# First attention of a four-part kernel: loads, statistics and moments of four batch entries in the set-up, those of the other 28 inside its first four steps, mask row on ScalarE

## What is computed

```python
x = x + _L0_xattn_ref(ctx_1024, _layernorm(x, axis=-1), mask, ...)   # the stage changed here
x = x + _L0_ffn_ref(_layernorm(x, axis=-1), ...)
x = x + _L1_xattn_ref(_layernorm(x, axis=-1), ctx_1024, ctx_1024, ...)
x = x + _L1_ffn_ref(x, ...)                # latent attention and a mixture of experts

def _L0_xattn_ref(x, latents, mask, ...):  # x is the context here, latents the tokens
    x, latents = layer_norm(x, ...), layer_norm(latents, ...)
    q = latents @ Wq
    k, v = split(concat([x, latents]) @ Wkv)
    q, k = l2norm(q) * q_scale, l2norm(k) * k_scale          # per head
    sim = where(full_mask, (q @ k.T) * 8, max_neg)           # mask over the 120 context keys
    return layer_norm((softmax(sim) @ v) @ Wo, ln_o_w, ln_o_b)
```

## Time and profile before

| | us |
|---|---|
| median of three runs (lowest, highest) | 1343.3 (1341.84, 1346.9) |
| the profiled execution | 1344.71 |
| its span, first to last instruction | 1342.9 |
| PE busy | 1228.8 (92%) |
| DVE busy | 927.4 (69%) |
| ACT busy | 798.7 (59%) |
| POOL busy | 590.4 (44%) |

### The profile page before, as it was taken

The page is one execution under the profiler, slowest core; times in us unless marked ns, Lnnn a source line. Parts: engine busy times, 40 slices in busy tenths (PEclk is TensorE's granted clock), DMA queues, the critical chain, the costliest instruction groups (busy, mean ns, idle before and its releaser), DMA issues. The chain is left out here.

```text
span 1342.9 us, 37984 instructions
## 1 busy us (share of the span) xinstructions
PE 1228.8 (92%) x13719; PEld 879.0 (65%) x13719; DVE 927.4 (69%) x1995; ACT 798.7 (59%) x2101; POOL 590.4 (44%) x677
## 2 busy tenths in 40 slices
PE   1799999999999995969999999599999979999996
PEld 0466666666666663437777777488888847777775
DVE  6476776776776773757989989399999956333431
ACT  0578778778778862216777777266666633333332
POOL 3587566566566555013233232543333224333343
PEclk9899999999999997988999999599999979999998
DMA  8000000000000000000000000200000000000000
GB/s 210 17 1 1 0 0 0 0 0 0 0 0 0 0 1 1 0 6 10 10 7 11 10 7 6 64 3 0 0 0 0 2 1 9 9 8 8 8 10 16
DMA packets 22740, 14.71 MB, mean 11 GB/s; under 512 B 6378, under 2 KB 21610, under 8 KB 22540
## 3 DMA queue, kind: packets, MB, share of 16 engines
q1 hardware_dynamic: 22520, 13.75, 3.9%
q10 hardware_dynamic: 148, 0.01, 0.0%
HBM read 11.66 MB, written 2.10 MB: 10 GB/s over the span
## 5 line engine op out<-in xcount | busy, mean ns | idle before, releaser
L694 POOL TENSOR_TENSOR r_norm<-ssm,mhalf 128x24 f32<-128x24 f32 x32 | 134.9, 4214 | 161.5 <-DVE ssm L599 161.5
L1938 ACT ACTIVATE moe_hid<-psum 128x512 f32<-128x512 f32 x128 | 76.4, 598 | 137.9 <-PE psum L1872 137.9
L537 ACT ACTIVATE l_probs<-psum,l_n_max 128x248 f32<-128x248 f32 x256 | 117.2, 481 | 57.5 <-DVE l_n_max L617 57.5
L2096 POOL TENSOR_TENSOR moe_acc<-moe_acc,moe_prod 128x512 f32<-128x512 f32 x64 | 81.3, 1271 | 147.8 <-DVE moe_prod L2052 147.8
L1882 PEld LDWEIGHTS psum<-w,moe_hid 128*128 128x128 f32 x1024 | 123.1, 192 | 27.0 <-issue 27.0
L2052 DVE TENSOR_TENSOR moe_prod<-psum,moe_combine 128x512 f32<-128x512 f32 x64 | 44.3, 692 | 136.2 <-PE psum L1882 136.1
L1882 PE MATMUL psum<-w,moe_hid 128*128 128x128 f32 x1024 | 123.4, 275 | 0.0
L1872 PE MATMUL psum<-moe_moe_hT,w 128*128 128x512 f32 x256 | 122.9, 608 | 0.0
L1726 POOL TENSOR_TENSOR mla_QX<-mla_qT,own_slots 128x512 f32<-128x512 f32 x32 | 33.3, 1042 | 136.0 <-ACT mla_qT L1560 136.0
L701 POOL TENSOR_TENSOR qkn<-qk,r_norm 128x1536 f32<-128x1536 f32 x32 | 88.4, 2762 | 2.5
L1726 POOL TENSOR_TENSOR l_QX<-l_qT,own_slots 128x512 f32<-128x512 f32 x32 | 33.3, 1042 | 122.3 <-ACT l_qT L1560 122.3
(11 more groups left out here) (311 smaller groups left out, 3393.2 us busy)
## 6 DMA issues: line engine op xcount, KB each, us to landing
X<-x_in SPq DMA_DIRECT2D x8, 256.0 KB, 4.9
out_dram<-moe_acc SPq DMA_DIRECT2D x32, 64.0 KB, 1.5
CT<-ctx_in SPq DMA_DIRECT2D x8, 240.0 KB, 6.1
l_cT<-ctxT_in SPq DMA_DIRECT2D x32, 60.0 KB, 1.8
w<-w_in SPq DMA_DIRECT2D x1, 1024.0 KB, 5.0
wm<-wm_in SPq DMA_DIRECT2D x1, 768.0 KB, 4.5
wp<-wp_in SPq DMA_DIRECT2D x1, 768.0 KB, 6.6
wkv<-wkv_in SPq DMA_DIRECT2D x1, 512.0 KB, 5.7
```

Source lines behind the costliest of these rows:

```text
L537: e = act.activation(probs[u][:, h, :], psum[:, 2 * u + h // 2, (h % 2) * K:(h % 2 + 1) * K], ACT.Exp, bias=n_max[u][:, h:h + 1], accum_ou ...
L694: pool.tensor_tensor(r_norm[:, :], ssm[:, :], mhalf[:, 0:3 * H], ALU.pow).then_inc(s["norm_inverted"], 1)
L1938: act.activation(hid[i % RING][:, :], psum[:, 2 + i % BANKS, :], ACT.Silu).then_inc(activated[i], 1)
L2096: pool.tensor_tensor(a[:, :, :], a[:, :, :], prod[e % 2][:, :, :], ALU.add).then_inc(summed[e], 1)
```

## The change

The loads go out in another order: group 0 of X and of CT, the weights, then the groups 1 to 7 of both in turn. The first block takes statistics and moments of entries 0 to 3 alone. A new function `later_stats(n)` ends DVE's body in steps -2, -1, 0 and 1 and does the same for seven entries each. POOL's later_scales waits for the variances of its seven. The mask row is made by ACT in the first block. POOL clears 32 partitions of one third of qk in place of all of sq and qk.

```diff
             @block.sync
-                for g in range(NG):
+                def load(g):
                     sp.dma_start(X[:, g * GB:(g + 1) * GB, :], ...).then_inc(x_loaded[g], 16)
-                for g in range(NG):
                     sp.dma_start(CT[0:C, g * GB:(g + 1) * GB, :], ...).then_inc(c_loaded[g], 16)
+
+                load(0)
                 sp.dma_start(wq[:, :], wq_in).then_inc(weights_loaded, 16)
...
+                for g in range(1, NG):
+                    load(g)
                 sp.wait_ge(weights_loaded, 80)
             @block.scalar
                 act.dma_start(cols[:, :], cols_in).then_inc(cols_loaded, 16)
+                act.wait_ge(keep_loaded, 32)
+                act.wait_ge(keep_zeroed, 1)
+                for r in (0, 64):
+                    act.activation(keep_row[r:r + 1, :, 0:C], keep8[r:r + 1, :].rearrange("a (b c) -> a b c", b=B), ACT.Copy,
+                                   bias=NEG_MAX, scale=-NEG_MAX)
             @block.gpsimd
-                pool.memset(sq[:, :, :], 1.0)
-                pool.memset(qk[:, :, :], 1.0)
+                pool.memset(qk[96:P, 1, :], 1.0).then_inc(zeroed, 1)
+                pool.wait_ge(zeroed, 3)
+                pool.wait_ge(var_ready, 1)
+                inverse_roots(pool, rstd, small[:, 0, :], mhalf, slice(0, FIRST)).then_inc(scales_made, 1)
                 pool.wait_ge(var_ready, 2)
-                inverse_roots(pool, rstd, small[:, 0, :], mhalf, slice(0, FIRST)).then_inc(scales_made, 1)
                 inverse_roots(pool, rstd_c[0:C], small_c[0:C, 0, :], mhalf, slice(0, FIRST)).then_inc(scales_made, 1)
             @block.vector
-                (bn_stats and moments of 32 entries of X, then of CT, and the mask row)
+                (the same for entries 0 to 3, and no mask row)
...
+                def later_stats(n):
+                    if isinstance(n, int) and n < 2:
+                        first = FIRST + CHUNK * (n + 2)
+                        some = slice(first, first + CHUNK)
+                        for b in range(first, first + CHUNK):
+                            dve.wait_ge(x_loaded[b // GB], 16)
+                            dve.bn_stats(stats6[:, b, :], X[:, b, :]).then_inc(x_stats_taken, 1)
+                        dve.wait_ge(x_stats_taken, first + CHUNK)
+                        variances_x(dve, some, n + 3)
+                        for b in range(first, first + CHUNK):
+                            dve.wait_ge(c_loaded[b // GB], 16)
+                            dve.bn_stats(stats6_c[0:C, b, :], CT[0:C, b, :]).then_inc(c_stats_taken, 1)
+                        dve.wait_ge(c_stats_taken, first + CHUNK)
+                        variances_c(dve, some, n + 3)
...
                     x_moments(n - 2)
+                    later_stats(n)
...
                 def later_scales(n):
                         some = slice(FIRST + CHUNK * (n + 1), FIRST + CHUNK * (n + 2))
+                        pool.wait_ge(var_ready, 2 * (n + 3))
```

More of the change, by code:

```diff
@@ L194, in l0_attention, with variances_x, variances_c @@
         later_weights_loaded = sem("later_weights_loaded")
+        def variances_x(dve, some, round_):
+            moments(dve, stats6, mean, small, x_moments_step, some, 6 * round_)
+            dve.tensor_scalar(small[:, 0, some], small[:, 3, some], 1.0 + LN_EPS, LN_EPS * LN_EPS, ALU.mult, ALU.add).then_inc(var_ready, 1)
+        def variances_c(dve, some, round_):
+            moments(dve, stats6_c[0:C], mean_c[0:C], small_c[0:C], c_moments_step, some, 6 * round_)
+            dve.tensor_scalar(small_c[0:C, 0, some], small_c[0:C, 3, some], LN_EPS, None, ALU.add).then_inc(var_ready, 1)
         with nc.Block() as block:
@@ L241, in _ @@
             def _(dve):
[L242 to L258, removed]
+                for b in range(FIRST):
+                    dve.wait_ge(x_loaded[0], 16)
+                    dve.bn_stats(stats6[:, b, :], X[:, b, :]).then_inc(x_stats_taken, 1)
+                dve.wait_ge(x_stats_taken, FIRST)
+                variances_x(dve, slice(0, FIRST), 0)
+                for b in range(FIRST):
+                    dve.wait_ge(c_loaded[0], 16)
+                    dve.bn_stats(stats6_c[0:C, b, :], CT[0:C, b, :]).then_inc(c_stats_taken, 1)
+                dve.wait_ge(c_stats_taken, FIRST)
+                variances_c(dve, slice(0, FIRST), 0)
                 dve.wait_ge(row_zeroed, 1)
                 dve.memset(first_row[64:65, :], 1.0)
[L261 to L264, removed]
                 dve.wait_ge(cols_loaded, 16)
@@ L855, in make_constants, with moments @@
                 n += 1
[L858 to L869, removed]
+def moments(dve, stats6, mean, small, step, some=slice(0, B), base=0):
+    m_even, v_even, m_odd, v_odd = (stats6[:, some, i] for i in (1, 2, 4, 5))
+    dve.tensor_tensor(small[:, 0, some], m_even, m_odd, ALU.add)
+    dve.tensor_tensor(small[:, 1, some], m_even, m_odd, ALU.subtract)
+    dve.tensor_tensor(small[:, 2, some], v_even, v_odd, ALU.add).then_inc(step, 3)
+    dve.wait_ge(step, base + 3)
+    dve.tensor_scalar(mean[:, some], small[:, 0, some], 0.5, None, ALU.mult).then_inc(step, 1)
+    dve.scalar_tensor_tensor(small[:, 3, some], small[:, 1, some], 0.25, small[:, 1, some], ALU.mult, ALU.mult).then_inc(step, 1)
+    dve.wait_ge(step, base + 5)
+    dve.scalar_tensor_tensor(small[:, 3, some], small[:, 2, some], 1.0 / D, small[:, 3, some], ALU.mult, ALU.add).then_inc(step, 1)
+    dve.wait_ge(step, base + 6)
 def entries(n, count=1):
```

## The result

The changed kernel takes 1361.55 us (median of 4 runs, 1360.8 to 1362.94); the kernel before took 1343.91 beside it (4 runs, 1341.84 to 1346.9). The ratio is 1.013, 95% interval 1.0118 to 1.0143: slower by 17.6 us, where 20.5 were forecast.

The account below looks back on a forecast made before the run. PE's queue bounds the steady steps, DVE then SP the set-up. -9.6 + 15.8 + 6.8 + 7.5 = +20.5 us on a median of 1343.3 gives 1363.8; own range 1358 to 1368, 8 in 10 1353 to 1371.

Parts of the forecast that it names:

- The earlier start: Set-up: SP's last issue still ends at 16.77, so the second block starts at 17.1 instead of 26.73 us; -9.6 us.
- Step -2: From the second block's start to the first insert in DVE's body: 11.75 us before, forecast change 0.
- The inserts' hold: Steps -2 to 2: DVE inserts of 5.2 us delay ln_c, and PE waits; 3.2 + 3 x 4.2 = 15.8 us.
- The waits for POOL: In the four inserts, the first two-input moments instruction waits until POOL's qkn ends; sum 6.8 us, lower bound 0.
- rival "no wait": The moments' seven-element operands slip in beside POOL without waiting; +13.7, 1357.0 us; chance 0.17.
- the rival built on it: POOL's power r_norm also blocks DVE, making the moments of X wait in each insert; +29.5, 1372.8 us; chance 0.08.
- The clock: PE's idling in steps 0 to 2 drops its clock to 1.2 GHz; three stalls lose 2.5 us each, 7.5 us.
- The rest: From step 3's first ln_x to the end of the span, experts' stage included: forecast change 0.

Follow-up runs that it names:

- two inserts of fourteen: Against the changed kernel: later statistics in two inserts of 14 entries, steps -2 and -1, behind norm_inputs, instead of four of seven; 1337.17 us, ratio 0.9949.
- single inputs: Against the changed kernel: moments of entries 4 to 31 from the even columns alone, each instruction with one SBUF operand; 1362.12 us, ratio 1.0135.
- the loads behind the barrier: Against the changed kernel: groups 1 to 7 of both inputs issued at the start of SP's second block; 1355.02 us, ratio 1.0084.
- reductions: Against the changed kernel: small instructions over later entries became one-element reductions from the even half, variance unscaled; 1360.73 us, ratio 1.0128.
- filler: Against the changed kernel: four unread 512-column matmuls on PE ahead of the turns in each of steps 0 to 2; 1358.2 us, ratio 1.0108.

## Why the prediction came out as it did

**The bound, the direction and the place** were right: PE's queue sets the pace, work on DVE ahead of what PE's turn waits for is paid but for 1.3 to 1.9 us of slack in each step, and it is not repaid. That the place is the cause is shown by the two inserts of fourteen: the same work, no stall and no fall of the clock in steps 0 to 2.

**The earlier start, -9.6, was -6.7.** The step that failed is "Bytes and rate are unchanged, so I leave its end at 16.77". The bytes of all loads together are the same, but neither the rate was, nor what had gone through by SP's last issue. The windows from 2 us to the end of SP's issuing, before and after, with GB/s at the end of each:

```profile
2.00:16.77 14.77, 0.00 (x0) 0.00 (x0) 11.42 (x58) 0.00 (x0) 6.23 (x6) 1.00 1.12 271
2.00:19.49 17.49, 0.00 (x0) 0.00 (x0) 3.85 (x24) 8.08 (x3) 6.16 (x7) 1.00 1.09 254
```

The rate was 254 GB/s instead of 271, and by the last issue 4.4 MB had gone through instead of 4.0. How the 2.7 us divide is told by the kernels with the same first block, whose rates differ (over 2 to 18.16 us): the one with inserts of fourteen had 272 GB/s, the rate of before, and SP was done at 18.16; the one with single inputs had 248 GB/s and SP was done at 19.79. At an equal rate the new order thus costs about 1.4 us, the other 1.3 us are the rate of this execution. A likely reason for the 1.4, not shown, is what is left in the queue behind SP's last issue. Before, the weights came last, and the very last load, of 128x128, took 0.43 us to issue. In the new order groups of 128x4x128 and 120x4x128 are last, and each holds SP for 0.8 to 1.26 us.

**Step -2, 0, was +1.2.** I took PE's projections there to last as before. They are limited by the speed of PE, and in this execution that came up later. PE's timeline before:

```profile
33.22 1.13 PE L349 MATMUL psum<-wkv,kvT 128*128 128x512 f32 x2 [0.68 <-ACT qk L508]
```

and after:

```profile
26.81 2.07 PE L357 MATMUL psum<-wkv,kvT 128*128 128x512 f32 x2 [0.67 <-ACT qk L516]
```

The same pair takes nearly twice as long. From PE's first matmul to the first pair at full speed it was 5.7 us before and about 11 after; it was 6.0 in the kernel with the loads behind the barrier and about 10 with the inserts of fourteen. In the kernel with reductions, whose instructions and loads are those of the changed kernel up to the first insert, it was 5.9 us and the step took 11.87. So the +1.2 does not follow from the change alone: of four kernels with the same instructions up to there (the changed one and those with single inputs, reductions and filler) three took 12.97 us and one 11.87. The granted clock in the windows reads 1.00 over these stretches (20.80 to 31.40 in the changed kernel), so it doesn't show this, and what decides it stays open.

**The inserts' hold, 15.8, was about 13.1.** That is what is left of the four steps (25.3 us) without the waits (7.1) and the half clock (5.2). The insert itself was mis-sized, 4.8 us and not 5.2: small instructions over 7 elements take 0.16 us, not the 0.2 of those over 32. That is about 1.5 of the 2.7; the rest is slack that I had put too low, 1.0 us where steps 0 to 2 had 1.3 to 1.5. The 13.1 is a remainder, and an error in the clock's 5.2 would move it the other way.

**The waits for POOL, 6.8, were 7.1** (2.53, 1.94, 1.28 and 1.32), at the instructions and to the ends that were forecast. The reason given, two inputs from SBUF, was wrong as a condition: one input waits as long. The row that the term was read from the earlier trace rows is itself a tensor_scalar, with one tile of 8 columns and two operands read per partition. What the runs show is that tensor_tensor, scalar_tensor_tensor and tensor_scalar over 7 or more columns wait beside qkn, while bn_stats and tensor_reduce don't. The Trainium skill (SBUF - State Buffer, Who interferes with whom) states that tensor_scalar in a mode that uses two ports and a DVE instruction with both inputs in SBUF contend with GpSimd, and that tensor_reduce never does on this chip; the waits agree with it, though no row shows which mode the tensor_scalar ran in. Had I used that rule, the rival "no wait" would have had less than its 0.17. The page's further statement that the first engine holds the ports for its whole instruction does not hold for r_norm, beside which the moments of X kept their 0.16 us from 34.50 to 35.30; the rival built on it is out.

**The clock, 7.5, was 5.2.** It fell behind all three stalls, as forecast, but PE did 4.0, 3.3 and 3.0 us of work at half rate, not 5.07. The case I sized it by, is PE resuming after a stage boundary; behind the stalls inside the pipeline PE did less before the clock came back. The filler gave 2.4 us of it back in steps 1 and 2.

**The rest, 0, was -1.6**, of which 1.4 lie in the experts' stage, where the half-clock stretch behind a pause of the same 6.01 us was shorter. No part of the change touches that stage, and over the ten profiled executions the unchanged part differs by up to 3.8 us; the -1.6 is not told apart from that.

The sum: -6.7 + 1.2 + 13.1 + 7.1 + 5.2 - 1.6 = +18.3, against 18.2 between the spans and 17.6 between the medians. In the forecast of +20.5 the losses of hold and clock were 5.0 us too large, the waits 0.3 too small, the gain was 2.9 too large, and step -2 and the rest weren't in it (-0.4 together), so that the errors partly cancelled: that the sum came within 2.3 us is in part luck. The low end of the forecast's own range, 1358, doesn't follow either: its terms' bounds taken halfway add up to 9.2 us below the forecast, which is 1355.

## What to carry to other kernels

Work that is taken out of a set-up must land where its engine waits in any case, and behind what the bounding engine needs next: the same 56 statistics with their moments made this kernel 17.6 us slower at the end of four bodies and 7.5 us faster behind norm_inputs of two. Before you move work into a step, look at what stands directly behind it in its queue, and at what the neighbouring engine is doing at that moment: if an instruction that waited there is replaced by one that doesn't, the next one that must wait takes over what is left of the wait. And a barrier waits for issues, not only for work: put loads that nobody needs yet behind it, but not so many that the first steps wait for them.

## What the runs showed of the hardware

SP's issuing of the same 21 loads ended at 16.77 us with the small ones last and at 18.16 to 19.95 us in seven executions with the large ones last; at an equal 271 to 272 GB/s it was 16.77 and 18.16. A wait beside POOL goes by the kind of the DVE instruction: 2.5 us for a tensor_scalar over 7 columns, 0 for a tensor_reduce over the same 7 and for bn_stats. It also goes by what POOL does: a multiplication over 1536 columns (2.76 us) holds DVE, a power over 24 columns (4.2 us) doesn't; whether the operation or the number of columns decides is not told apart. ACT's pass from bytes to bf16 over 3840 elements of one partition takes 3.40 us, against the 2.15 that DVE needs. PE ran its first projections at half speed for 6 to 11 us while the granted clock read 1.00, and the length differed between executions of the same instructions.
